# Turning the expert tiles' rows: DMA transposes on SyncE's queue in place of TensorE's, in a kernel of gated cross attention and a mixture of experts

## The chip, the cores and the metric

The kernel runs on one core of one Trainium2 chip. The metric is the device time of one execution in microseconds (us). A core has five engines that run at their own pace and meet at semaphores: TensorE (PE, matmuls and transposes, results in PSUM), VectorE (DVE), ScalarE (ACT), GpSimd (POOL) and SyncE (SP), which here only issues DMAs. Sixteen DMA engines move the data.

## The reference

```python
x = x + xattn(layernorm(x), ctx, ctx, ...)   # gated attention with decay, 8 heads, sequences of 128
x = x + ffn(layernorm(x), gate_w, w1, b1, w2, b2)

def ffn(x, gate_w, w1, b1, w2, b2):          # 4096 tokens, D=256, F=1024, 8 experts, the best 2 of them
    gate_scores = softmax(xf @ gate_w)
    topk_scores, topk_idx = top_k(gate_scores, 2)
    topk_scores = topk_scores / sum(topk_scores)
    h = gelu(einsum('td,edf->etf', xf, w1) + b1)
    y = einsum('etf,efd->etd', h, w2) + b2
    out = einsum('kt,ktd->td', topk_scores.T, y_sel)   # y_sel: y of the chosen experts
```

All arrays are float32.

## The kernel before

The kernel has two parts. In the first, up to about 250 us, eight steps of four sequences each go through the attention; each ends with the normed rows of 256 values and 16 more fields (token, gates) being scattered into a table in DRAM, `expert_rows`, sorted by expert. In the second part, which overlaps the last steps of the first, 39 tiles of table rows go through their expert: tiles 0 to 31 have 256 rows (`R`), tiles 32 to 38 have 128 that count.

Every engine has its own program, written out in order by hand; semaphores join them. There is no scheduler. Tile t passes through these stages:

- SP loads its rows (272 values each, `ROW`) from the table into one of four slots `xg[k]`, k = t mod 4 (`load`, the DMA on L523): three slots lie in `weight_stage`, the fourth in `v_centred_and_one`. Which rows, it reads from a list in SBUF, `rowi`.
- TensorE turns them: four 128x128 float32 transposes (two for a half tile) into PSUM (`turn_rows`, L1504), since layer 1 wants the 256 values along the partitions.
- DVE splits the turned rows into a high and a low float16 half (`split_rows`): a cast (L2087) and a subtraction (L2089), from PSUM into `xh[t mod 2]`, in the trace `x_slots`. The products of the halves give near float32 accuracy: three matmuls for one.
- TensorE does layer 1, 48 matmuls (L1519) into the bank group `scores`; ScalarE applies gelu in four quarters (L1038); DVE splits the result (L2096, L2098); TensorE does layer 2, 48 matmuls (24 for a half tile, L1533); DVE adds the bias and multiplies by the gate (L2105, L2111); POOL adds the rows to `out_rows` in DRAM by an indirect DMA (L663).

A "turn" t is one round of the tile loop: on TensorE it is the transposes of tile t+1, layer 1 of tile t and layer 2 of tile t-1, in this order; on DVE it is the split and the fields of tile t+1 (`row_fields`), the four gelu splits of tile t and the gating of tile t-1. So on DVE the split of tile t+1 comes behind the gating of tile t-2, which needs the end of TensorE's turn t-1. Turns 0 to 12 and the last ones are written out, 13 to 28 are a loop. Between the turns of DVE lie the routing of the last two attention steps (`choose`, `records`) and the list of the late tiles (`late_list0` to `late_list2`, between turns 6 and 9).

SP's program between its row loads: `write_x1(LAST)` writes the last attention result; after `next_rows(8)` come nine `clear`s (L488, 272 KB of zeros each, into the table's unused rows), then waits for the late list (`s_tl2`), for all scatters and for all clears (`s_clear`), then `next_rows(9)`. In the kernel before `next_rows(n)` loads tile n+4 as soon as tile n has been turned (`s_xT`) and its fields are read (`s_id`).

In code, the clears stand here:

```python
for n in range(3, EARLY - 4):        # EARLY = 13
    next_rows(n)
... # nine clears
sp.wait_ge(s_tl2, 2)
... # all scatters landed
sp.wait_ge(s_clear, 16 * (NE + 1))
for n in range(EARLY - 4, EARLY):
    next_rows(n)
```

Of the kernel before, what the change touches and what calls it, by code (L numbers as in the profile page):

```python
# [13 lines left out]
P = 128  # L14
R = 2 * P
# [32 lines left out]
def build(nc, x, ctx_in, igate_w, igate_b, fgate_w, fgate_b, out_w, gate_w, w1, b1, w2, b2, out):  # L48
# [51 lines left out]
    with ExitStack() as ctx:  # L100
# [3 lines left out]
        def sem(name):  # L104
            return ctx.enter_context(nc.semaphore(name))
# [249 lines left out]
        x_slots = [stage[:, :, :].rearrange("p a f -> p (a f)")[:, s * SLOT:(s + 1) * SLOT] for s in range(3)]  # L355
        xg = [x.rearrange("p (b w) -> p b w", w=ROW) for x in x_slots + [v_old[:, 0:SLOT]]]
        hf = E[:, 0:2, :, :].rearrange("p a c t -> p (a c t)")
        hh = [x.rearrange("p (w c t) -> p w c t", w=2, c=FC) for x in (
# [14 lines left out]
        s_xhi = sem("rows_high")  # L373
        s_xh = sem("row_halves")
        s_l1 = sem("layer1_quarter")
# [9 lines left out]

        L20, Y0, FREE0 = 1, 4, 3

        class Turn:
# [11 lines left out]
            def slot(self, ahead):  # L400
                return (self.u + ahead) % 4

            def landed(self, ahead, dmas=1):
# [10 lines left out]
        with nc.Block() as block:  # L414

            @block.sync
            def _(sp):
# [107 lines left out]

                def next_rows(t):
                    tr = Turn(0, t)
                    sp.wait_ge(s_xT, t + 1)
                    sp.wait_ge(s_id, t + 1)
                    load(tr, 4)  # L530

                def turn(tr, first, left):
                    if left > 4:
                        sp.wait_ge(s_xT, tr.t + 1)
                        sp.wait_ge(s_id, tr.t + 1)
                        load(tr, 4)

                write_x1(NEXT_LAST)
# [12 lines left out]
                next_rows(0)  # L551
                next_rows(1)
                next_rows(2)
                write_x1(LAST)
                for n in range(3, EARLY - 4):
                    next_rows(n)
# [549 lines left out]
            def _(pe):  # L1106
# [392 lines left out]
                run_steps(body, pe)  # L1499
                def turn_rows(tr, ahead):  # L1500
                    pe.wait_ge(s_gx[tr.slot(ahead)], tr.landed(ahead))
                    for c in range(KC):
                        for b in range(tr.rows(ahead) // P):
                            ins = pe.transpose(ps_xt[:, c * R + b * P:c * R + b * P + P],  # L1504
                                               xg[tr.slot(ahead)][:, b, c * P:(c + 1) * P], ident[:, :])
                    ins.then_inc(s_xT, 1)
# [36 lines left out]
                def tile_turn(tr, first, left, beside=()):  # L1543
# [9 lines left out]
                    if left > 0:  # L1553
                        expert = expert_of(tr.t)
                        pe.wait_ge(s_xh, tr.t + 1)
                        if left > 1:
                            turn_rows(tr, 1)
                        for q in range(4):
                            layer1(tr, expert, first, (q,))
                            routing()  # L1560
# [12 lines left out]
                pe.wait_ge(s_ee, NSTEP * (2 * SB))  # L1573
                turn_rows(Turn(0, 0), 0)
                stream_before(last, 3, 3)
# [16 lines left out]
            def _(dve):  # L1592
# [476 lines left out]
                def row_fields(tr, ahead):  # L2069
# [48 lines left out]
                def turn(tr, first, left, beside=()):  # L2118
                    if first:
                        row_fields(tr, 0)  # L2120
                        split_rows(tr, 0)
                    else:
                        expert = dve.value_load(exi[0:1, bass.ds(tr.t - 1, 1)], min_val=0, max_val=NE - 1)
                    if left > 1:
                        if not first:
                            dve.wait_ge(s_l1, tr.t * 4)
# [19 lines left out]
                row_fields(Turn(0, 0), 0)  # L2146
                split_rows(Turn(0, 0), 0)
                h_norm(last)
# [48 lines left out]
```

## Time and profile before

| | |
|---|---|
| median of three timed runs | 671.48 us (670.55 to 677.57) |
| span of the profiled execution, first to last instruction | 672.2 us |
| TensorE busy with matmuls | 626.9 us, 93% of the span |
| VectorE | 489.8 us, 73% |
| ScalarE | 323.3 us, 48% |
| GpSimd | 187.1 us, 28% |
| mean granted TensorE clock | 0.981 |

The profile comes from one execution; for it the page gives the span and no time of its own, so the span stands for it. Times in timelines count from its first instruction. Busy shares are means over stages that have different limits: in the attention all engines wait for each other in turn, in the tile loop from about 300 us on TensorE hardly pauses. Matmuls overlap in the array, and their ends are modelled, so the distance between starts says more than a row's own duration.

### The profile page before, as it was taken

The numbers are of one execution on the slowest core, as the hardware profiler recorded it, in microseconds if no ns is written. First come the engines' busy times: TensorE is split into PE (matmuls) and PEld (weight loads), VectorE is DVE, ScalarE is ACT, GpSimd is POOL, SyncE is SP. The second block draws the span as 40 slices with busy tenths as digits, with TensorE's granted clock in tenths as the row PEclk, the third lists the DMA queues.
The fourth block names the chain that finished last, engine by engine and source line by source line (L and its number), as shares of the span: only waits on it lengthen the run. The fifth ranks groups of instructions, "written<-read, shape, count | busy, mean of one in ns | idle before, by whom it ended". The sixth has DMA issues, their size and how long they took to land. (4 is left out here: it accounts for less than half of the span.)

```text
span 672.2 us, 20373 instructions
## 1 busy us (share of the span) xinstructions
PE 626.9 (93%) x6736; PEld 533.2 (79%) x6737; DVE 489.8 (73%) x1330; ACT 323.3 (48%) x767; POOL 187.1 (28%) x185
## 2 busy tenths in 40 slices
PE   1799998999889899999999999999999999999985
PEld 1567876778677668988989898988889898988774
DVE  2457988979889898985889866757675757666562
ACT  2668888777878746543332232323232323232321
POOL 3000003231323315135345332313141323233112
PEclk9899999969999999999999999999999999999998
DMA  4534537654644636333374423233232323133100
GB/s 139 156 106 148 160 94 231 188 189 144 207 152 137 199 103 208 77 70 78 66 221 93 68 40 61 43 56 46 46 52 44 57 39 64 35 65 53 21 4 1
DMA packets 55036, 66.55 MB, mean 99 GB/s; under 512 B 5472, under 2 KB 50720, under 8 KB 54832
## 3 DMA queue, kind: packets, MB, share of 16 engines
q1 hardware_dynamic: 41552, 48.13, 24.1%
q0 software_dynamic: 13296, 17.32, 14.1%
q8 instruction: 49, 0.80, 0.5%
q14 instruction: 27, 0.22, 0.1%
q10 hardware_dynamic: 112, 0.08, 0.1%
HBM read 41.50 MB, written 24.92 MB: 99 GB/s over the span
## 5 line engine op out<-in xcount | busy, mean ns | idle before, releaser
L1038 ACT ACTIVATE decay_slots<-scores,b_turned 128x256 f32<-128x256 f32 (+1 forms) x312 | 124.4, 451 | 257.4 <-PE scores L1519 244.9
L1519 PE MATMUL scores<-x_slots,w_halves 128*128 128x256 f16 (+1 forms) x1872 | 203.3, 264 | 0.8 <-issue 0.8
L1519 PEld LDWEIGHTS scores<-x_slots,w_halves 128*128 x1872 | 173.4, 98 | 23.3 <-issue 1.4
L641 POOL DMA_INDIRECT expert_rows<-xf_rows,slot_i x64 | 66.7, 1042 | 224.1 <-issue 114.8
L1533 PE MATMUL pv<-w_halves,decay_slots 128*128 x864 | 97.7, 273 | 0.0
L663 POOL DMA_INDIRECT out_rows<-v_centred_and_one,row_ids x36 | 57.8, 1605 | 138.8 <-DVE v_centred_and_one L2111 96.1
L1533 PE MATMUL gate_bank<-w_halves,q_and_k_halves 128*128 x840 | 95.0, 273 | 0.0
L1533 PEld LDWEIGHTS pv<-w_halves,decay_slots 128*128 128x128 f16 x864 | 84.1, 98 | 10.5 <-issue 0.3
L1533 PEld LDWEIGHTS gate_bank<-w_halves,q_and_k_halves 128*128 128x128 f16 x840 | 81.8, 98 | 10.1
L663 POOL DMA_INDIRECT out_rows<-work,row_ids x35 | 55.3, 1580 | 112.1 <-DVE work L2111 84.7
L1257 PEld LDWEIGHTS pv<-v_centred_and_one,decay_slots 128*128 128x128 f32 x512 | 64.5, 197 | 1.6
L1257 PE MATMUL pv<-v_centred_and_one,decay_slots 128*128 128x33 f32 x512 | 64.7, 262 | 0.0
L2098 DVE TENSOR_TENSOR decay_slots<-decay_slots 128x512 f16<-128x512 f32 (+1 forms) x80 | 51.2, 640 | 2.7
L2098 DVE TENSOR_TENSOR q_and_k_halves<-decay_slots,q_and_k_halves 128x512 f16<-128x512 f32 (+1 forms) x76 | 49.5, 652 | 2.6
L1705 DVE SCALAR_TENSOR_TENSOR w_halves<-weight_stage,w_halves 128x1024 f16<-128x1024 f32 x32 | 38.9, 1219 | 10.5 <-ACT w_halves L780 10.3
L768 ACT ACTIVATE decay_slots<-turn_bank 128x512 f32<-128x512 f32 x64 | 38.2, 597 | 10.7 <-PE turn_bank L1153 9.5
L1714 DVE SCALAR_TENSOR_TENSOR decay_slots<-scores,decay_slots 128x1024 f32<-128x1024 f32 x32 | 39.1, 1222 | 4.6 <-PE scores L1200 3.2
L2087 DVE CAST x_slots<-turn_bank 128x512 f16<-128x512 f32 (+1 forms) x39 | 25.1, 643 | 17.9 <-PE scores L1519 10.2
L1255 PE MATMUL pv<-minus_big_above,ident_bf 128*128 128x240 bf16 x128 | 34.9, 273 | 2.7 <-ACT work L789 1.6
L2096 DVE CAST decay_slots<-decay_slots 128x512 f16<-128x512 f32 (+1 forms) x80 | 33.5, 419 | 5.1 <-ACT decay_slots L1038 4.0
L780 ACT ACTIVATE w_halves<-weight_stage 128x1024 f16<-128x1024 f32 x32 | 33.7, 1055 | 3.4 <-DMA weight_stage<-in_L_ffn_w 3.4
L2096 DVE CAST q_and_k_halves<-decay_slots 128x512 f16<-128x512 f32 (+1 forms) x76 | 32.4, 426 | 1.2 <-ACT decay_slots L1038 0.8
(257 smaller groups left out, 845.5 us busy)
## 6 DMA issues: line engine op xcount, KB each, us to landing
weight_stage<-in_L_ffn_w SPq DMA_DIRECT2D x32, 512.0 KB
x_slots<-in_x SPq DMA_DIRECT2D x16, 512.0 KB
weight_stage<-expert_rows SPq DMA_DIRECT2D x30, 272.0 KB
ctx_slots<-in_ctx SPq DMA_DIRECT2D x8, 512.0 KB
out_rows<-x_slots SPq DMA_DIRECT2D x8, 512.0 KB
v_centred_and_one<-expert_rows SPq DMA_DIRECT2D x9, 272.0 KB
expert_rows<-v_centred_and_one SPq DMA_DIRECT2D x9, 272.0 KB
expert_rows<-xf_rows,slot_i POOLq DMA_INDIRECT x64
```

Of the source, the lines that this page charges most:

```text
L641: pool.indirect_dma_start(table, bass.IndirectOffsetOnAxis(ap=sloti[:, step[1], j, k:k + 1], axis=0), xfn[:, step[1], j, :], None, bounds_ ...
L663: pool.indirect_dma_start(out_rows, bass.IndirectOffsetOnAxis(ap=ids[:, k, b:b + 1], axis=0), yo[k][:, b, :], None, bounds_check=T - 1, oo ...
L768: act.activation(E[:, j, HG * r:HG * r + HG, :].rearrange("p c s -> p (c s)"), ps_t[:, :], ACT.Exp).then_inc(s_ee, 1)
L1038: ins = act.activation(hf[:, f * R:f * R + tr.rows(0)], ps_s[:, q, n * R:n * R + tr.rows(0)], ACT.Gelu, bias=b1T[:, bass.ds(expert, 1), f] ...
L1255: pe.matmul(ps_h[:, P + P + 16:512], ident_h[:, :], never[:, 0:120].unsqueeze(1).broadcast_to([P, 2, 120]), start=True, stop=True)
L1257: ins = pe.matmul(ps_h[:, h * (DH + 1):(h + 1) * (DH + 1)], E[:, j, k * KC + u, :], vaug[:, step[1], j, h, :], start=True, stop=True)
L1519: ins = pe.matmul(o, w, xh[:, tr.slot(0) % 2, b, k, 0:tr.rows(0)], start=(n == 0), stop=(n == 3 * KC - 1))
L1533: ins = pe.matmul(ps_y[k % 2][:, c * D:(c + 1) * D], hh[k % 2][:, a, f, c * P:(c + 1) * P], w, start=(f == 0 and n == 0 and c == 0), stop= ...
L1705: dve.scalar_tensor_tensor(out=lo, in0=stage[:, half, :], scalar=W_SCALE, in1=hi, op0=ALU.mult, op1=ALU.subtract).then_inc(s_lo, 1)
L1714: dve.scalar_tensor_tensor(out=c, in0=ps_s[:, :, 0:KC * P], scalar=QK_SCALE, in1=c, op0=ALU.mult, op1=ALU.mult).then_inc(s_cm, 1)
L2096: dve.tensor_copy(hi, src).then_inc(s_hhi, 1)
L2098: dve.tensor_tensor(lo, src, hi, ALU.subtract).then_inc(s_hh, 1)
```

## The change

The rows are now split as they lie, tokens along the partitions, and the float16 halves are turned afterwards. `split_rows` reads the slot `xg[k]` in SBUF, writes the high half into a buffer of its own (`xg_high`, two of them: the room of `out_w_rows`, which the attention no longer needs by then, and a spare piece of `weight_stage`) and the low half over the first part of the slot itself (`xg_low`). Then SP issues four DMA transposes a tile, each of 128 rows by 256 float16 values, from the two halves into `xh[t mod 2]`. Tile 0 alone still goes through TensorE. The halves are signalled by two semaphores `s_xh[0]` and `s_xh[1]`, 64 counts a tile. All tiles are split and turned at 256 rows, the last seven too. `next_rows(n)` on SP now first turns tile n+1, then loads tile n+4; `write_x1(LAST)` comes two calls earlier.

```diff
@@ names
+        xg_low = [x.bitcast(F16).rearrange("p (b w) -> p b w", w=2 * ROW)[:, :, 0:D]
+                  for x in x_slots + [v_old[:, 0:SLOT]]]
+        spare = stage[:, :, :].rearrange("p a f -> p (a f)")[:, 3 * SLOT:3 * SLOT + R // P * D // 2]
+        xg_high = [x.bitcast(F16).rearrange("p (b d) -> p b d", d=D) for x in (outw[:, :], spare)]
...
+        TURNED = 16 * 2 * (R // P)
...
+            def turned(self, ahead):
+                return (self.i * 2 + (self.u + ahead) // 2) * TURNED + TURNED
@@ SyncE
+                def turn_rows(tr, ahead):
+                    k = tr.slot(ahead)
+                    sp.wait_ge(s_xlo, tr.t + ahead)
+                    sp.sem_inc(s_held, 1)
+                    if not (isinstance(tr.t, int) and tr.t + ahead == 1):
+                        sp.wait_ge(s_l1, tr.t * 4 + (ahead - 1) * 4)
+                        sp.sem_inc(s_held, 1)
+                    for w, rows in enumerate((xg_high[k % 2], xg_low[k])):
+                        for b in range(R // P):
+                            sp.dma_start_transpose(out=xh[:, k % 2, w, :, b * P:b * P + P],
+                                                   in_=rows[:, b, :]).then_inc(s_xh[k % 2], 16)
+
+                def turn(tr, first, left):
+                    if left > 1:
+                        turn_rows(tr, 1)
+                    if left > 4:
+                        sp.wait_ge(s_xh[tr.slot(0) % 2], tr.turned(0))
+                        sp.sem_inc(s_held, 1)
+                        sp.wait_ge(s_id, tr.t + 1)
+                        sp.sem_inc(s_held, 1)
+                        load(tr, 4)
+
                 def next_rows(t):
-                    tr = Turn(0, t)
-                    sp.wait_ge(s_xT, t + 1)
-                    sp.wait_ge(s_id, t + 1)
-                    load(tr, 4)
...
+                    turn(Turn(0, t), False, NT)
...
                 next_rows(0)
-                next_rows(1)
-                next_rows(2)
                 write_x1(LAST)
-                for n in range(3, EARLY - 4):
+                for n in range(1, EARLY - 4):
                     next_rows(n)
@@ TensorE, tile_turn
-                        pe.wait_ge(s_xh, tr.t + 1)
-                        if left > 1:
-                            turn_rows(tr, 1)
+                        pe.wait_ge(s_xh[tr.slot(0) % 2], tr.turned(0))
@@ VectorE
                 def split_rows(tr, ahead):
-                    dve.wait_ge(s_xT, tr.t + (ahead + 1))
-                    n = tr.rows(ahead)
-                    src = ps_xt[:, :].rearrange("p (c t) -> p c t", c=KC)[:, :, 0:n]
-                    hi, lo = (xh[:, tr.slot(ahead) % 2, w, :, 0:n] for w in range(2))
+                    k = tr.slot(ahead)
+                    dve.wait_ge(s_gx[k], tr.landed(ahead))
+                    if not (isinstance(tr.t, int) and tr.t + ahead < 3):
+                        dve.wait_ge(s_xh[k % 2], tr.turned(ahead - 2))
+                    src, hi = xg[k][:, :, 0:D], xg_high[k % 2]
                     dve.tensor_copy(hi, src).then_inc(s_xhi, 1)
                     dve.wait_ge(s_xhi, tr.t + (ahead + 1))
-                    dve.tensor_tensor(lo, src, hi, ALU.subtract).then_inc(s_xh, 1)
+                    dve.tensor_tensor(xg_low[k], src, hi, ALU.subtract).then_inc(s_xlo, 1)
```

How the instructions stand at two places. First SP, behind the last clear (`expert_rows<-v_centred_and_one`). Before, the next instruction that waits is the row load of tile 13:

```order
L488 DMA expert_rows<-v_centred_and_one 128x2x272
L522 TENSOR_LOAD ctx_slots [waits rows_scattered11,empty_rows_cleared,rows_scattered10,rows_turned,rows_scattered01,ids_and_gates,rows_scattered00,late_tiles_listed]
L522 ISA x2
L523 ISA
L523 DMA weight_stage<-expert_rows 128x2x272
```

Now, in the same place, the transposes of tile 10 from its high half (`out_w_rows`) and its low half (`weight_stage`):

```order
L499 DMA expert_rows<-v_centred_and_one 128x2x272
L547 DMA_TRANSPOSE x_slots<-out_w_rows 128x2x128 [waits rows_scattered11,empty_rows_cleared,rows_scattered10,rows_low,rows_scattered01,late_tiles_listed,rows_scattered00,layer1_quarter]
L547 DMA_TRANSPOSE x_slots<-out_w_rows 128x2x128
L547 DMA_TRANSPOSE x_slots<-weight_stage 128x2x128 x2
L533 TENSOR_LOAD ctx_slots [waits row_halves_turned1,ids_and_gates]
L533 ISA x2
L534 ISA
L534 DMA weight_stage<-expert_rows 128x2x272
```

What moved: four transposes of tile 10 now stand between the clears and the row load, and the first of them carries the waits for clears, scatters and late list.

Second TensorE at the start of a turn: behind layer 2 (`pv` or `gate_bank`) it reads two entries of the expert list, then begins layer 1 (`scores`). Before:

```order
L1533 MATMUL pv<-w_halves,decay_slots 128x256 x4
L1541 TENSOR_LOAD ctx_slots
L1541 ISA x2
L1541 TENSOR_LOAD ctx_slots
L1541 ISA x2
L1504 MATMUL turn_bank<-ident,weight_stage 128x128 [waits rows_in1,row_halves]
L1504 MATMUL turn_bank<-ident,weight_stage 128x128 x3
L1519 ISA [waits gelu_quarter]
```

Now, at such a place:

```order
L1556 MATMUL gate_bank<-w_halves,q_and_k_halves 128x256 x4
L1564 TENSOR_LOAD ctx_slots
L1564 ISA x2
L1564 TENSOR_LOAD ctx_slots
L1564 ISA x2
L1542 ISA [waits gelu_quarter,row_halves_turned1]
L1542 MATMUL scores<-x_slots,w_halves 128x256 x2
```

What moved: the transposes are gone, and layer 1 itself waits for the landed halves of its tile.

## Rows read from the trace of the kernel before

**Rows 1.** The page: its first line.
```profile
span 672.2 us, 20373 instructions
```

**Rows 2.** Windows: PE, PEld, DVE, ACT, POOL busy; granted clock, DMA share, GB/s.
```profile
450.00:500.00 50.00, 49.95 (x458) 44.75 (x457) 32.05 (x75) 14.25 (x34) 13.06 (x9) 1.00 0.26 43
```

**Rows 3.** Groups by form, 284 to 606 us: two casts.
```profile
L2096 DVE CAST q_and_k_halves<-decay_slots 128x512 f16<-128x512 f32 x60 | 27.0, 450 | 0.1
...
L2087 DVE CAST x_slots<-turn_bank 128x512 f16<-128x512 f32 x28 | 19.4, 692 | 13.3 <-PE scores L1519 10.0 <-issue 2.3 <-DVE ctx_slots L2043 0.9
```

**Rows 4.** Timeline of a steady turn (start, duration, engine, line).
```profile
486.52 5.40 PE L1519 MATMUL scores<-x_slots,w_halves 128*128 128x256 f16 x48
...
489.87 1.55 POOL L663 DMA_INDIRECT out_rows<-work,row_ids  x1 [0.30 <-issue]
...
497.00 0.60 PE L1504 MATMUL turn_bank<-ident,v_centred_and_one 128*128 128x128 f32 x4
...
497.44 5.40 PE L1519 MATMUL scores<-x_slots,w_halves 128*128 128x256 f16 x48
...
499.76 0.69 DVE L2089 TENSOR_TENSOR x_slots<-turn_bank,x_slots 128x512 f16<-128x512 f32 x1
```

**Rows 5.** Timeline of the first turns, 254 to 286 us.
```profile
254.65 0.46 SPq L550 DMA_DIRECT2D q_and_k_halves<-in_L_ffn_b  x1
...
258.38 0.69 DVE L2089 TENSOR_TENSOR x_slots<-turn_bank,x_slots 128x512 f16<-128x512 f32 x1
...
262.18 0.63 PE L1504 MATMUL turn_bank<-ident,weight_stage 128*128 128x128 f32 x4 [0.43 <-issue]
...
269.46 0.69 DVE L2089 TENSOR_TENSOR x_slots<-turn_bank,x_slots 128x512 f16<-128x512 f32 x1
...
273.95 0.60 PE L1504 MATMUL turn_bank<-ident,v_centred_and_one 128*128 128x128 f32 x4
...
281.42 0.69 DVE L2089 TENSOR_TENSOR x_slots<-turn_bank,x_slots 128x512 f16<-128x512 f32 x1
...
285.26 0.60 PE L1504 MATMUL turn_bank<-ident,weight_stage 128*128 128x128 f32 x4
```

**Rows 6.** DMA issues: KB each and median us from issue to landing.
```profile
q_and_k_halves<-in_L_ffn_b SPq DMA_DIRECT2D x1, 1024.0 KB, 6.4
...
out_rows<-work,row_ids POOLq DMA_INDIRECT x35, 3.8
```

**Rows 7.** Timeline of turns 7 to 10: queue, splits, transposes.
```profile
338.90 0.38 SPq L523 DMA_DIRECT2D weight_stage<-expert_rows  x1
...
339.32 10.52 SPq L488 DMA_DIRECT2D expert_rows<-v_centred_and_one  x9
...
343.62 0.60 PE L1504 MATMUL turn_bank<-ident,weight_stage 128*128 128x128 f32 x4
...
350.83 0.69 DVE L2089 TENSOR_TENSOR x_slots<-turn_bank,x_slots 128x512 f16<-128x512 f32 x1
...
365.89 5.40 PE L1519 MATMUL scores<-x_slots,w_halves 128*128 128x256 f16 x48
```

**Rows 8.** Windows around the end of the clears.
```profile
350.00:352.00 2.00, 2.00 (x21) 1.80 (x19) 1.82 (x6) 0.49 (x2) 0.81 (x1) 1.00 0.62 215
```

**Rows 9.** Windows: granted clock after a stretch in which PE was idle.
```profile
26.81:28.60 1.79, 0.01 (x1) 0.00 (x0) 1.65 (x7) 1.57 (x4) 0.00 (x0) 1.00 0.76 262
28.60:29.23 0.63, 0.00 (x0) 0.00 (x1) 0.56 (x3) 0.13 (x1) 0.00 (x0) 0.51 0.16 54
29.23:35.00 5.77, 5.77 (x26) 4.39 (x27) 1.20 (x1) 2.97 (x6) 0.00 (x0) 0.50 0.31 91
```

**Rows 10.** Timeline of two of the last turns (tiles of 128 rows).
```profile
647.17 4.19 PE L1519 MATMUL scores<-x_slots,w_halves 128*128 128x128 f16 x48
...
648.52 0.42 DVE L2089 TENSOR_TENSOR x_slots<-turn_bank,x_slots 128x256 f16<-128x256 f32 x1
...
654.95 4.32 PE L1519 MATMUL scores<-x_slots,w_halves 128*128 128x128 f16 x48 [0.78 <-issue]
```

More of the change, by code:

```diff
@@ L373, in build @@
         s_xhi = sem("rows_high")
-        s_xh = sem("row_halves")
+        s_xlo = sem("rows_low")
+        s_xh = [sem(f"row_halves_turned{k}") for k in range(2)]
         s_l1 = sem("layer1_quarter")
@@ L524, in load @@
                         s_gx[k], 16)
-                def next_rows(t):
-                    tr = Turn(0, t)
-                    sp.wait_ge(s_xT, t + 1)
-                    sp.wait_ge(s_id, t + 1)
-                    load(tr, 4)
[L532 to L536, printed above, removed]
+                def turn_rows(tr, ahead):
[18 more added lines that the diff above has]
+                        load(tr, 4)
+                def next_rows(t):
+                    turn(Turn(0, t), False, NT)
                 write_x1(NEXT_LAST)
@@ L1499, in _, with turn_first_rows @@
                 run_steps(body, pe)
-                def turn_rows(tr, ahead):
-                    pe.wait_ge(s_gx[tr.slot(ahead)], tr.landed(ahead))
+                def turn_first_rows():
+                    pe.wait_ge(s_gx[0], 16)
                     for c in range(KC):
-                        for b in range(tr.rows(ahead) // P):
+                        for b in range(R // P):
                             ins = pe.transpose(ps_xt[:, c * R + b * P:c * R + b * P + P],
-                                               xg[tr.slot(ahead)][:, b, c * P:(c + 1) * P], ident[:, :])
+                                               xg[0][:, b, c * P:(c + 1) * P], ident[:, :])
                     ins.then_inc(s_xT, 1)
@@ L1573, in _ @@
                 pe.wait_ge(s_ee, NSTEP * (2 * SB))
-                turn_rows(Turn(0, 0), 0)
+                turn_first_rows()
                 stream_before(last, 3, 3)
@@ L2080, in row_fields, with split_first_rows @@
                     dve.tensor_tensor(gate[:, k, :], xg[k][:, :, F_SECOND], part[:, k, :], ALU.subtract).then_inc(s_id, 1)
-                def split_rows(tr, ahead):
-                    dve.wait_ge(s_xT, tr.t + (ahead + 1))
-                    n = tr.rows(ahead)
-                    src = ps_xt[:, :].rearrange("p (c t) -> p c t", c=KC)[:, :, 0:n]
-                    hi, lo = (xh[:, tr.slot(ahead) % 2, w, :, 0:n] for w in range(2))
+                def split_first_rows():
+                    dve.wait_ge(s_xT, 1)
+                    src = ps_xt[:, :].rearrange("p (c t) -> p c t", c=KC)
+                    hi, lo = (xh[:, 0, w, :, :] for w in range(2))
+                    dve.tensor_copy(hi, src).then_inc(s_xhi, 1)
+                    dve.wait_ge(s_xhi, 1)
+                    dve.tensor_tensor(lo, src, hi, ALU.subtract).then_inc(s_xh[0], TURNED)
+                def split_rows(tr, ahead):
+                    k = tr.slot(ahead)
[3 more added lines that the diff above has]
+                    src, hi = xg[k][:, :, 0:D], xg_high[k % 2]
                     dve.tensor_copy(hi, src).then_inc(s_xhi, 1)
                     dve.wait_ge(s_xhi, tr.t + (ahead + 1))
-                    dve.tensor_tensor(lo, src, hi, ALU.subtract).then_inc(s_xh, 1)
+                    dve.tensor_tensor(xg_low[k], src, hi, ALU.subtract).then_inc(s_xlo, 1)
                 def split_gelu(tr, q):
@@ L2118, in turn @@
                 def turn(tr, first, left, beside=()):
[L2119 to L2122, printed above, removed]
+                    if not first:
                         expert = dve.value_load(exi[0:1, bass.ds(tr.t - 1, 1)], min_val=0, max_val=NE - 1)
                     if left > 1:
-                        if not first:
-                            dve.wait_ge(s_l1, tr.t * 4)
                         split_rows(tr, 1)
@@ L2146, in _ @@
                 row_fields(Turn(0, 0), 0)
-                split_rows(Turn(0, 0), 0)
+                split_first_rows()
                 h_norm(last)
```

## The prediction, made before the changed kernel ran

> **What bounds the kernel now.** I read the windows first. In the steady turns TensorE (PE) is busy 49.95 of 50 us at a granted clock of 1.00, VectorE (DVE) 32.05, ScalarE 14.25, and the DMA engines have a share of 0.26 [rows 2]. So from 300 us on the end is set by what TensorE has to do, and its transposes are part of that. Then the timeline of one turn [rows 4]: layer 1 starts at 486.52 and again at 497.44, a turn of 10.92 us; the four transposes of the next tile's rows start at 497.00 and hold the array until 497.44, 0.44 us. Their end is modelled, so the gap to the next matmul is what counts, not the 0.60 of the row. In the same turn the low half of the split is done at 499.76 + 0.69 = 500.45, 3.45 us after the transposes start. Third, the timeline of the first turns and of turns 7 to 10, where DVE has routing and tile lists to work out and its split comes late [rows 5, 7]. Times are those of the profiled execution, whose span is 672.2 us [rows 1]; the timed median is 671.48, 0.7 less, and I take that off at the end.
>
> **What goes from TensorE.** Tiles 1 to 31 lose four transposes each, 31 x 0.44 = 13.6 us. Tiles 32 to 38 (128 rows, two transposes) lose at most half of that each; part of it lies in the pause that stays at the start of those turns (0.78 us before the turn at 654.95, which has no transposes at all [rows 10]), so I count 1.2 us for the seven. With everything hidden the change is worth 14.8 us: 656.7.
>
> **What the split costs.** The cast of 128x512 read PSUM in 692 ns; casts of that size from SBUF take 450 [rows 3], so each split ends 0.24 us earlier after it starts. The subtraction stays at 0.69. DVE is not the bound in a steady turn, so this only gives the transposes more time. In the last seven turns the split now handles 256 rows instead of 128: 0.45 + 0.69 instead of 0.42 + 0.42, 0.3 us longer beside idle DVE time.
>
> **What the DMA transposes cost.** No row shows one. Call q the time that the SyncE queue is held by one of 64 KB, and T the time from the end of the split to the landing of all four. For q the nearest row is the plain load from the same queue, 0.38 us [rows 7]; that is the low end. The high end is an indirect DMA whose descriptors GpSimd builds, 1.55 [rows 4] (its landing is 3.8 [rows 6]). For landing after the last issue: the nine clears stop issuing at 339.32 + 10.52 = 349.84, and in 350 to 352 the DMA share is 0.62, so traffic ends near 351.6, 1.8 us later [rows 7, 8]; the high end is 3.8. That gives T from 4 x 0.39 + 1.8 = 3.4 to 4 x 1.55 + 3.8 = 10.0. I take q = 0.6 and 2.2 for landing, **T = 4.6**: near the plain row, since queue and issuing engine are the same, and above it, since a plain copy is the least that a transposing one can be.
>
> Two pages of the Trainium skill point opposite ways. "VectorE: DVE Perf Modes", section "The three transpose paths", gives 1309 ns for a 128x128 transpose by DMA and 390 for one by TensorE; a tile has eight such blocks, one after the other an estimate of 10.5 us, which is the slow rival below; the trace has TensorE at 0.44 for all of a tile's f32 blocks. "DMA: Bandwidth & Descriptors", section "Latency and other measured facts", gives an effective 261 GB/s for transposes, so that a tile's 256 KB would move in an estimated 1.0 us and only issue and landing would count. No row of before decides between them.
>
> **Steady turns.** A turn becomes 10.48 us. The split ends 3.45 - 0.24 = 3.2 us into it, so the transposes have 7.3 us before layer 1 wants them. At T = 4.6 nothing waits. The row load of the tile three turns later, now behind the transposes on the queue, has turns to spare. Where T is over 7.3, layer 1 of a tile starts (3.2 + T) after the turn before the last ended, so two turns take 10.48 + 3.2 + T.
>
> **First turns.** Tile 1: the split would end near 258.8, and SyncE has just issued the 1 MB bias load, which lands 6.4 us after 254.65 [rows 5, 6]; by T or behind that load the halves are there at about 263.4, wanted at 262.18. From there turn 1 takes 273.95 - 262.18 - 0.44 = 11.3, so turn 2 starts layer 1 at 274.7 (before: 273.95 + 0.44 = 274.4); tile 2's halves are there at 270.15 - 0.5 + 4.6 = 274.3. Turn 3: 285.6 by TensorE, but tile 3's split ends at 282.11 - 0.24, and 4.6 later it is 286.5, against 285.7 before. So turn 4 starts about 0.4 us later than before instead of 1.8 earlier; turns 4 to 7 then gain 0.44 each: turn 8 starts **1.4 us earlier**.
>
> **Turn 10, the wait that the change adds.** SyncE's program has nine clears of 272 KB between the transposes of tile 9 and those of tile 10, and behind them it waits for the late tile list, all scatters and all clears. In before only row loads stood behind this, four tiles ahead. Now tile 10's transposes do, and layer 1 of turn 10 waits for them. In the time of the trace before, with turn 8 starting at 343.62 [rows 7]: tile 9's split ends at 351.52 - 0.24 = 351.28; four transposes 2.4 us; the load of tile 12 1.2 (10.52 / 9, what a lookup and an issue take among the clears); the first clear at 354.9; from first clear to last landing 351.6 - 339.3 = 12.3, so 367.2; then T: 371.8. Without a wait turn 10 would start at 343.62 + 2 x 10.48 = 364.6. **Stall: 7.2 us** (1.5 or so of it already at turn 9, whose halves come at 351.28 + 4.6 = 355.9, wanted at 354.1). Between the bounds of q and T it is 5.2 to over 11. What is late next is nothing: DVE and ScalarE catch up during the stall.
>
> A stall of this length also costs clock. TensorE is idle from 26.81 to 29.23; the granted clock is 1.00 until 28.6, 0.51 in the rest of the pause, and 0.50 for the 5.8 us of work from 29.23 to 35 [rows 9], the lower of its two levels, 1.2 GHz of 2.4. Layer 1 is dense matmuls, so 6 us at half speed do 3 us of work: **+3.0** (0 if the clock holds).
>
> **Sum.** Start of turn 10: -1.4 - 2 x 0.44 + 7.2 = +4.9; clock +3.0, so +7.9. Turns 10 to 30: 21 x 0.44 = -9.2. Last seven -1.2. Total **-2.5 us**: 669.7 for the profiled execution, 671.48 - 2.5 = **669.0** for the median.
>
> **Rivals.**
> A. The short one: q = 0.39, T = 3.4, clock unharmed. Turn 8 starts 2.6 earlier, the stall is 369.8 - 364.6 = 5.2, and 2.6 + 0.9 - 5.2 + 9.2 + 1.2 = 8.7 us are won: 662.8. Were the wait for the clears hidden altogether, it would be 656.7. For it: the DMA engines have 0.26 of share in a steady turn. Against it: the wait stands in the program order, and the clears alone are 12.3 us.
> B. Longer transposes, still inside a turn: q = 1.1, T = 7.0. First turns +2.8 at turn 4, +1.0 at turn 8, stall 11.6, clock 3: +14.7 at turn 10, -9.2 after. The last turns take 7.78 us now (647.17 to 654.95 [rows 10]) and split at 648.52 + 0.42; there two turns are 7.6 + 2.2 + 7.0, so 8.4 each, +3. Total +8.5: 680.
> C. Slower, by one mechanism: the chain split, four transposes, layer 1 is longer than the turn's 7.3 us and takes TensorE's place as the bound. It decides from T = 7.3. At T = 10.0, the top of the row bounds, two turns take 23.7, so +0.9 a turn instead of -0.4: about +7 in the first turns, +4 in turns 4 to 7, +15 from the stall, clock 3, +19 in turns 10 to 30, +13 in the last seven: +61, 732. At T = 8.5 the same sum gives about 705. For it: nothing shows what a transposing DMA takes, and the two accumulates of each turn (3.8 us to land) run just when it would. Against it: 7.3 us is more than any issue and landing of the plain rows add up to.
> D. That it doesn't do what it says: if the transposes' landing were hidden but TensorE's 0.44 us were only turned into another wait at the turn's start, nothing but the stall (371.8 against 365.5) and its clock would be left: 671.5 + 6.3 + 3.0 = 681. The steady windows (no idle TensorE, no wait named) speak against it.
>
> **Chances.** Forecast (T 4 to 5.5, stall and clock as above, 665 to 673) 0.40; A 0.25; B and times between it and the forecast 0.15; C 0.17; D 0.03. About 1% is what a measurement of this kernel can tell from no change, 664.8 to 678.2. Faster by more: A, 0.25. Within: the forecast and a third of B, 0.45. Slower: 0.30. The range must leave out at most 0.2: below, A's better half under 660 (0.06); above, the part of C from T = 8.5 (0.12). So 660 to 703.
>
> **What the profile after would show.** Right: layer 1 starts every 10.48 us between 400 and 600; four transposing DMAs on SyncE's queue after each split, landed well before the turn ends; one idle TensorE stretch of 5 to 8 us around 366, released by a DMA into the tile halves, with a granted clock of 0.5 behind it; waits of about 1 us at the starts of turns 1 and 3. Wrong: no idle stretch at turn 10 (the clears' wait was hidden), an idle TensorE before every tile (C), or a queue held over 1 us by a transpose (B). I would be most wrong by q, which enters T four times and the stall eight times.

## The result, and the profile of the changed kernel

The changed kernel takes 696.42 us (median of 4 runs, 694.34 to 699.54) against 671.98 us of the kernel before (4 runs beside it): a ratio of 1.0351, 95% interval 1.03 to 1.0402. It is 3.5% slower. The forecast of 669.0 was wrong in sign; the time lies inside the range.

The profiled execution took 699.54 us, its span is 697.5. A run's time was 2.0 us above its span here and in the runs below, so I compare spans with spans: 697.5 - 672.2 = +25.3 us. By the medians it is 24.4. The four executions of the changed kernel have spans from 692.3 to 697.5, and the profiled one is the longest. The head of the page, its DMA line, its costliest group and its sum over the groups of waits:

```profile
span 697.5 us, 20366 instructions
...
PEclk9899997999979998999999799999999999999998
...
DMA packets 98813, 76.54 MB, mean 110 GB/s; under 512 B 49248, under 2 KB 94496, under 8 KB 98608
...
L1542 PE MATMUL scores<-x_slots,w_halves 128*128 128x256 f16 (+1 forms) x1872 | 212.0, 272 | 32.4 <-DMA x_slots<-weight_stage 29.1
```

The waits of TensorE from 250 us on (in total, times, longest):

```profile
PE scores L1542 <- DMA x_slots<-weight_stage: 29.1, 12, 10.0
PE scores L1542 <- DMA x_slots<-v_centred_and_one: 1.9, 2, 1.6
```

Layer 1 waits 31 us for transposed halves, in 14 of 38 turns. The answer to [rows 4] is the timeline of a steady turn (start, duration):

```profile
500.47 0.69 DVE L2119 TENSOR_TENSOR weight_stage<-weight_stage 128x512 f16<-128x512 f32 x1
...
501.57 4.92 SPq L547 DMA_TRANSPOSE x_slots<-weight_stage  x4
...
507.63 0.40 SPq L534 DMA_DIRECT2D weight_stage<-expert_rows  x1
508.83 5.13 PEld L1542 LDWEIGHTS scores<-x_slots,w_halves 128*128 x48 [0.39 <-issue]
...
519.21 0.86 PEld L1542 LDWEIGHTS scores<-x_slots,w_halves 128*128 x8
519.32 0.93 PE L1542 MATMUL scores<-x_slots,w_halves 128*128 128x256 f16 x7
```

From 508.83 to 519.32 it is 10.49 us. The four transposing DMAs hold the queue for 4.92 us, 1.23 each; the plain load of 272 KB takes 0.40. From the end of the split (501.16) to the start of layer 1 (508.83) it is 7.7 us, but that is the slack and not T: no wait for a transpose is named here, and the 0.39 of waiting is no wait for one either. The run with two transposing DMAs a tile (e1_half, below) has the same 0.39 at its turn 21, with its transposes off the queue 5.0 us before:

```profile
483.66 2.33 SPq L547 DMA_TRANSPOSE x_slots<-weight_stage  x2
...
490.97 1.10 PEld L1542 LDWEIGHTS scores<-x_slots,w_halves 128*128 x11 [0.39 <-issue]
```

T can be read where layer 1 does wait for a transpose. In those 14 turns it starts 6.5 to 8.2 us after the split (turn 10: after the first issue), 7.1 in the middle: 5.0 to 6.5 us in which the four DMAs hold the queue, and 1.2 to 2.1 us from the end of the last issue. The forecast had 4.6.

The windows against [rows 2]: the DMA share is 0.48 in place of 0.26, and TensorE works 49.04 of 50 us; what is missing are the waits of turns 16 and 17 (0.73 and 0.23).

```profile
450.00:500.00 50.00, 49.04 (x448) 43.50 (x447) 32.07 (x77) 14.51 (x35) 15.98 (x9) 1.00 0.48 78
```

Turn 1, against [rows 5]: the bias load is issued at 254.88, the transposes behind it take 6.11 us, layer 1 starts at 267.03. Under it the windows around this (PE, PEld, DVE, ACT, POOL busy; granted clock; DMA share; GB/s):

```profile
259.18 6.11 SPq L547 DMA_TRANSPOSE x_slots<-weight_stage  x4
...
267.03 2.74 PE L1542 MATMUL scores<-x_slots,w_halves 128*128 128x256 f16 x12 [5.57 <-DMA x_slots<-weight_stage]
```

```profile
261.00:267.00 6.00, 0.46 (x5) 0.16 (x2) 5.83 (x9) 2.84 (x8) 3.00 (x3) 0.79 0.45 102
267.00:272.00 5.00, 4.97 (x28) 3.44 (x29) 0.89 (x2) 1.77 (x5) 1.57 (x3) 0.57 0.65 216
272.00:274.00 2.00, 2.00 (x39) 1.84 (x38) 1.69 (x4) 1.13 (x3) 0.00 (x0) 1.00 0.00 0
```

Turns 9 and 10, against [rows 7]: the transposes of tile 9, the nine clears, the transposes of tile 10.

```profile
359.64 0.69 DVE L2119 TENSOR_TENSOR weight_stage<-weight_stage 128x512 f16<-128x512 f32 x1
...
360.50 5.05 SPq L547 DMA_TRANSPOSE x_slots<-weight_stage  x4
...
366.67 0.39 SPq L534 DMA_DIRECT2D weight_stage<-expert_rows  x1
...
367.11 11.43 SPq L499 DMA_DIRECT2D expert_rows<-v_centred_and_one  x9
...
367.17 6.90 PE L1542 MATMUL scores<-x_slots,w_halves 128*128 128x256 f16 x48 [3.53 <-DMA x_slots<-weight_stage]
...
371.87 0.69 DVE L2119 TENSOR_TENSOR weight_stage<-weight_stage,out_w_rows 128x512 f16<-128x512 f32 x1
...
382.48 2.77 SPq L547 DMA_TRANSPOSE x_slots<-out_w_rows  x2
...
385.30 2.54 SPq L547 DMA_TRANSPOSE x_slots<-weight_stage  x2
...
389.32 2.95 PE L1542 MATMUL scores<-x_slots,w_halves 128*128 128x256 f16 x13 [10.01 <-DMA x_slots<-weight_stage]
```

```profile
379.30:389.30 10.00, 0.01 (x1) 0.00 (x0) 2.82 (x9) 0.00 (x0) 3.10 (x2) 0.73 0.62 105
389.30:395.00 5.70, 5.68 (x31) 4.19 (x32) 1.12 (x2) 1.20 (x3) 0.00 (x0) 0.57 0.41 97
395.00:396.00 1.00, 1.00 (x11) 0.90 (x10) 0.45 (x2) 0.53 (x3) 0.00 (x0) 1.00 0.05 4
```

Tile 10's split is done at 372.56 and its transposes are issued at 382.48. Of the waits that stand between, the one for the clears to land ended last (SyncE's own waits: in total, times, longest):

```profile
SPq L589 <- DMA expert_rows<-v_centred_and_one: 3.6, 1, 3.6
```

TensorE is idle for 10.01 us and then runs 5.7 us at a granted clock of 0.57. Of the last turns, against [rows 10], one of the long waits:

```profile
679.76 4.88 PE L1542 MATMUL scores<-x_slots,w_halves 128*128 128x128 f16 x48 [2.57 <-DMA x_slots<-weight_stage]
```

**Where the 25.3 us are.** From the start of layer 1 of one turn to that of another, after less before (turn 0 starts at 254.88 and 255.08, turn 38 at 679.76 and 654.95):

| turns | before | after | difference |
|---|---|---|---|
| start of turn 0 | 255.08 | 254.88 | -0.2 |
| 0 to 4 | 41.54 | 49.38 | +7.8 |
| 4 to 5 | 13.36 | 15.76 | +2.4 |
| 5 to 8 | 34.08 | 32.96 | -1.1 |
| 8 to 10 | 21.83 | 36.34 | +14.5 |
| 10 to 11 (low clock) | 10.92 | 12.83 | +1.9 |
| 11 to 31 | 218.92 | 212.06 | -6.9 |
| 31 to 38 | 59.22 | 65.55 | +6.3 |
| 38 to the end | 17.25 | 17.74 | +0.5 |

### The profile page after: what moved, and what is told of

It reads as the page before. It is cut to its first block and busy times, and to the rows that moved or that the text cites. A ratio compares the mean times of both kernels' runs of the same rounds, so it can differ in the third digit from the quotient of the medians.

```text
span 697.5 us, 20366 instructions
## 1 busy us (share of the span) xinstructions
PE 626.3 (90%) x6598; PEld 526.4 (75%) x6599; DVE 485.5 (70%) x1330; ACT 324.2 (46%) x767; POOL 196.0 (28%) x185
## 2 busy tenths in 40 slices
DMA packets 98813, 76.54 MB, mean 110 GB/s; under 512 B 49248, under 2 KB 94496, under 8 KB 98608
## 5 line engine op out<-in xcount | busy, mean ns | idle before, releaser
L1542 PE MATMUL scores<-x_slots,w_halves 128*128 128x256 f16 (+1 forms) x1872 | 212.0, 272 | 32.4 <-DMA x_slots<-weight_stage 29.1
L1542 PEld LDWEIGHTS scores<-x_slots,w_halves 128*128 x1872 | 177.6, 101 | 63.1 <-issue 38.9
L686 POOL DMA_INDIRECT out_rows<-v_centred_and_one,row_ids x36 | 61.4, 1707 | 163.4 <-DVE v_centred_and_one L2141 117.1
L1556 PE MATMUL pv<-w_halves,decay_slots 128*128 x864 | 97.7, 273 | 0.2 <-issue 0.2
L1556 PE MATMUL gate_bank<-w_halves,q_and_k_halves 128*128 x840 | 96.0, 273 | 0.7 <-issue 0.6
L1556 PEld LDWEIGHTS pv<-w_halves,decay_slots 128*128 128x128 f16 x864 | 84.2, 98 | 10.4 <-issue 0.3
L1556 PEld LDWEIGHTS gate_bank<-w_halves,q_and_k_halves 128*128 128x128 f16 x840 | 82.3, 98 | 11.2 <-issue 1.4
L686 POOL DMA_INDIRECT out_rows<-work,row_ids x35 | 59.3, 1694 | 106.7 <-DVE work L2141 79.6
L1280 PEld LDWEIGHTS pv<-v_centred_and_one,decay_slots 128*128 128x128 f32 x512 | 66.6, 202 | 1.7
L1280 PE MATMUL pv<-v_centred_and_one,decay_slots 128*128 128x33 f32 x512 | 66.7, 266 | 0.0
L2128 DVE TENSOR_TENSOR q_and_k_halves<-decay_slots,q_and_k_halves 128x512 f16<-128x512 f32 (+1 forms) x76 | 49.4, 650 | 2.6
L1169 PE MATMUL turn_bank<-pick_head,three_parts 96*128 96x512 bf16 x64 | 25.7, 401 | 4.3 <-DVE three_parts L1703 2.4
```

The source lines that it names most:

```text
L686: pool.indirect_dma_start(out_rows, bass.IndirectOffsetOnAxis(ap=ids[:, k, b:b + 1], axis=0), yo[k][:, b, :], None, bounds_check=T - 1, oo ...
L1280: ins = pe.matmul(ps_h[:, h * (DH + 1):(h + 1) * (DH + 1)], E[:, j, k * KC + u, :], vaug[:, step[1], j, h, :], start=True, stop=True)
L1542: ins = pe.matmul(o, w, xh[:, tr.slot(0) % 2, b, k, 0:tr.rows(0)], start=(n == 0), stop=(n == 3 * KC - 1))
L1556: ins = pe.matmul(ps_y[k % 2][:, c * D:(c + 1) * D], hh[k % 2][:, a, f, c * P:(c + 1) * P], w, start=(f == 0 and n == 0 and c == 0), stop= ...
L2128: dve.tensor_tensor(lo, src, hi, ALU.subtract).then_inc(s_hh, 1)
```

## The experiments

Single runs without rounds are compared by their spans with 697.5. The start of turn 0, which no edit here should move, lies between 248.7 and 256.5 us in the profiles, and the changed kernel's own spans differ by 5.2 us, of which 697.5 is the top. So one span says little below 5 us; distances between turns are steadier.

### The chain with two DMAs a tile in place of four

Only the high halves are turned, and layer 1 reads the high half where it would read the low one. So this kernel leaves out the low halves of the rows, and TensorE does as many matmuls as before.

```diff
-        TURNED = 16 * 2 * (R // P)
+        TURNED = 16 * (R // P)
-                    for w, rows in enumerate((xg_high[k % 2], xg_low[k])):
+                    for w, rows in enumerate((xg_high[k % 2],)):
...
-                                    ins = pe.matmul(o, w, xh[:, tr.slot(0) % 2, b, k, 0:tr.rows(0)], start=(n == 0),
+                                    ins = pe.matmul(o, w, xh[:, tr.slot(0) % 2, 0, k, 0:tr.rows(0)], start=(n == 0),
```

> Only the high halves are turned by DMA (two transposing DMAs a tile instead of four), and layer 1 multiplies the high half where it would take the low one, so the output leaves out the low halves of the rows; TensorE does as many matmuls as in the changed kernel. Theory Q (the time that four transposes hold SyncE's queue, 1.24 us each, plus 2.3 us of landing, is what layer 1 waits for): T falls from 7.3 to 4.8, the stalls of the last turns (6.3 us in sum against before) go, those of the first turns and of turns 9 and 10 shrink by 2.5 to 5 each: a span of 677 to 682. Rival W (only the place of the clears costs, the transposes' own length does not): the stall of turn 10 shrinks by at most 2.5 and the rest stays, 693 to 696.

Measured: 674.59 us, span 672.6, 24.9 less than the changed kernel and 4.4 below what was expected. On the queue, a pair takes 2.3 to 2.5 us:

```profile
547.19 2.31 SPq L547 DMA_TRANSPOSE x_slots<-weight_stage  x2
```

Layer 1 of turn 9 starts 4.0 us after its split, that of turn 10 3.7 us after the first issue: a T somewhat under the prediction's 4.6. From turn 8 to turn 10 this kernel takes 28.7 us (344.21 to 372.89); the prediction had 28.2 (343.62 to 371.8). The terms, measured against forecast: 11.5 against 11.3 us to the first clear, 13.5 against 12.3 from there to the transposes, 3.7 against 4.6 to layer 1. So the model of the stall held to about a microsecond a term, and what it was fed for the transposes did not.

### Per DMA or per byte

Eight DMAs of 128x128 (32 KB) move the same bytes:

```diff
-                            sp.dma_start_transpose(out=xh[:, k % 2, w, :, b * P:b * P + P],
-                                                   in_=rows[:, b, :]).then_inc(s_xh[k % 2], 16)
+                            for c in range(KC):
+                                sp.dma_start_transpose(out=xh[:, k % 2, w, c, b * P:b * P + P],
+                                                       in_=rows[:, b, c * P:c * P + P]).then_inc(s_xh[k % 2], 16)
```

> Eight transposing DMAs of 128x128 a tile instead of four of 128x256, the same bytes. If the queue is held per DMA (a fixed price of 1.24 us), T is 8 x 1.24 + 2.3 = 12.2, two turns take 10.48 + 3.2 + 12.2, 12.9 each, and the span is 770 to 800. If it is held per byte (0.62 us each), T and the span stay where they are, 695 to 700. In between: a fixed part f and a part by bytes, f = 2 x q(32 KB) - 1.24.

Measured: 817.55 us, span 815.6, above the 770 to 800 that a price per DMA was expected to give and far from the 695 to 700 of a price per byte. Four of them take 5.06 us, 1.27 each, for half the bytes of those above:

```profile
539.39 5.06 SPq L548 DMA_TRANSPOSE x_slots<-v_centred_and_one  x4
```

The other way: the high half of a tile in one DMA of 128x512 (128 KB), the low half in two as before.

```diff
+                        if w == 0:
+                            sp.dma_start_transpose(out=xh[:, k % 2, w, :, :, :].rearrange("p b c t -> p (b c) t"),
+                                                   in_=rows.rearrange("p b d -> p (b d)")).then_inc(s_xh[k % 2], 16)
```

> Three transposing DMAs a tile: the high half in one of 128x512 (128 KB), the low one in two as before. Layer 1 reads the tile in two pieces of 128 columns instead of 256 in a row. If the queue is held per DMA, T falls by 1.24 to 6.1 and the span to about 688; if per byte, the large one holds it 2.5 us and the span stays at 695 to 700.

Measured: 688.16 us, span 686.1. The 128 KB take 1.24 us (L547), the two of 64 KB behind them 1.26 each (L551):

```profile
547.57 1.24 SPq L547 DMA_TRANSPOSE x_slots<-out_w_rows  x1
548.86 2.52 SPq L551 DMA_TRANSPOSE x_slots<-weight_stage  x2
```

The span of 686.1 is near the 688 expected. A transposing DMA held the queue for 1.21 to 1.26 us in the median at 32, 64 and 128 KB alike; single ones took from 0.9 to 2.7. The price is per DMA. A price per byte is ruled out by both runs.

### Two DMAs a tile

The low half is packed without gaps in its slot, so each half goes in one DMA of 128x512.

```diff
-        xg_low = [x.bitcast(F16).rearrange("p (b w) -> p b w", w=2 * ROW)[:, :, 0:D]
+        xg_low = [x.bitcast(F16)[:, 0:R // P * D].rearrange("p (b d) -> p b d", d=D)
-        TURNED = 16 * 2 * (R // P)
+        TURNED = 16 * 2
```

> Two transposing DMAs a tile, one for each half (128x512, 128 KB each): the low half is written side by side at the start of its slot, so that each half is one row of 512 values in a partition. Same work, half the DMAs. The runs so far held the queue 1.24 to 1.27 us per DMA for 32, 64 and 128 KB alike, so T should fall from 7.3 to 2 x 1.25 + 2.3 = 4.8, as in the run with only the high halves: 673 to 677. If the landing of 128 KB takes clearly longer than that of 64 KB, 680 to 688.

Measured: 678.87 us (676.26 to 681.0, 4 runs), ratio to the kernel before 1.01 (1.006 to 1.0139), span 677.2. A tile's two transposes take 2.36 us:

```profile
571.92 2.36 SPq L546 DMA_TRANSPOSE x_slots<-weight_stage  x2
```

Two issues fewer a tile are worth 17.6 us by the medians (696.42 to 678.87); the time came out 2 us above what was expected. The waits for transposes that are left are 7.35 us at turn 10, 3.53 at turn 1, 2.51 at turn 7, 1.48 at turn 34, 1.21 at turn 9 and three under 0.8.

### Which tiles pay

In these kernels a list of tiles keeps TensorE's transposes, and so the order of before; the rest is the changed kernel with four DMAs a tile.

```diff
+        BY_PE = (0,) + tuple((9, 10))
...
-                    if left > 1:
+                    if left > 1 and not by_pe(tr, 1):
                         turn_rows(tr, 1)
...
@@ TensorE
                         pe.wait_ge(s_xh[tr.slot(0) % 2], tr.turned(0))
+                        if left > 1 and by_pe(tr, 1):
+                            turn_rows(tr, 1)
```

The other two lists are (1, 2, 3) and tiles 32 to 38. Tiles 9 and 10:

> The changed kernel (four DMAs a tile) with tiles 9 and 10 turned by TensorE. Theory: stalls of 3.5 and 10.0 us and some 3 us at the low clock go, a stall of about 3 at turn 11 comes, since tile 11's transposes are now the first behind the clears: 685 to 689. If the loss before turn 11 is only moved to another place, 693 or more.

Measured: 684.49 us, span 682.5, 15.0 less than the changed kernel, 2.5 below what was expected. From turn 8 to turn 12 it takes 48.7 us (351.80 to 400.49), the changed kernel 59.7 (352.98 to 412.63) and the kernel before 43.7: 11.0 of the 16.0 us that were lost there come back, and turn 11 now waits 3.54. The rest of the 15.0 lies in turns that are the same in both programs (turn 0 alone starts 2.7 us earlier). So the wait behind the clears, with its clock, is the largest single loss.

Tiles 1 to 3:

> Tiles 1, 2 and 3 keep TensorE's transposes beside tile 0; all others are turned by four transposing DMAs as in the changed kernel. Theory (each first turn pays for its own late transposes, and the wait at turn 10 is a thing apart): the loss of the first turns, 7.6 us by the start of layer 1 of turn 4, goes nearly whole, so the span falls from 697.5 to 689 to 692 us, with the wait of turn 10 still about 10 us. Rival (the first turns are late because four transposes of any tile do not fit beside the load of the first weights, and the lateness only moves to tile 4): the span stays at 694 to 698.

Measured: 689.39 us, span 687.4, 10.1 less, 1.6 below what was expected. From turn 0 to turn 4 it takes 42.4 us (256.50 to 298.86) against 49.4, 7.0 of the 7.8 back. Turn 4 to 5 takes 13.7 against 15.8, although tiles 4 and 5 are turned as in the changed kernel. The wait at turn 10 is 8.45 us. The lateness does not move on to tile 4, where 1.68 us are waited.

Tiles 32 to 38:

> Tiles 32 to 38 keep TensorE's transposes beside tile 0; all others are turned by four transposing DMAs. Theory (the short last turns cannot hold casts and four transposes of 1.24 us): the waits of the last turns, 2.3 to 2.6 us each in the changed kernel, go, and the span falls from 697.5 by 5 to 6 us to 691.5 to 693. Rival (something else of the last turns is late too, the rows' loads behind results on the queue): a fall under 2 us, 695.5 to 698.

Measured: 687.73 us, span 685.8, 11.7 less where 5 to 6 were expected. From turn 31 to the end it takes 75.1 us (610.68 to 685.8), the changed kernel 83.3, the kernel before 76.5: 8.2 are the tiles' own. The other 3.5 lie elsewhere, in turns that are the same in both programs (turn 0 starts 1.3 us earlier, turns 0 to 10 take 2.7 less), and are put down to the scatter between executions. The rival is ruled out.

All three groups together, with four DMAs elsewhere (tiles 1, 2, 3, 9, 10 and 32 to 38 by TensorE):

> Tiles 1, 2, 3, 9, 10 and 32 to 38 are turned by TensorE as before, the other 26 (4 to 8, 11 to 31) by DMA. Theory Q: the places where the split ends late or the turn is short are taken out, all the rest hides; 26 x 0.44 = 11.4 us of TensorE are saved, less some 2 us of small waits in the steady turns: 661 to 664, faster than both kernels. Rival B (DMA engines shared with row loads and accumulates slow every turn): no better than before, 670 to 676.

Measured: 672.32 us (669.87 to 679.18, 10 runs), ratio 1.0036 (0.9998 to 1.0075), span 667.9. Missed by 8 us at the median, by 4 in the profiled execution, which is the fastest of the ten (spans from 667.9 to 677.2); what the slower ones lose no profile shows. The time is the rival's, its mechanism is not seen: steady turns take 10.48 us here too. The first tile behind the clears is now tile 11, and turn 11 waits in turn 10's place. Its transposes on the queue, and its layer 1:

```profile
371.31 2.50 SPq L551 DMA_TRANSPOSE x_slots<-weight_stage  x2
373.85 2.55 SPq L551 DMA_TRANSPOSE x_slots<-v_centred_and_one  x2
```

```profile
378.35 7.03 PE L1546 MATMUL scores<-x_slots,w_halves 128*128 128x256 f16 x48 [3.02 <-DMA x_slots<-v_centred_and_one]
```

Two more waits of 1.75 and 1.30 us stand at tiles 4 and 6, T being 6.8 and 7.2 at turns 6 and 11.

### A version that is faster

Two DMAs a tile, and tiles 1, 2, 3, 9, 10 and 11 by TensorE:

> As the run with two DMAs a tile, but tiles 1, 2, 3, 9, 10 and 11 (late splits, and the clears on the queue) are turned by TensorE. T of 4.8 fits everywhere else; 25 x 0.44 + 1 us are saved, one wait of about 1 us in the last turns: 660 to 665, faster than both kernels. If contention on the DMA engines costs the rest, 669 to 673.

Measured: **664.35 us** (661.56 to 667.29, 6 runs), ratio to the kernel before 0.9892 (0.9858 to 0.9927), span 662.5. It beats both kernels, the one before by 1.1%. Waits for transposes are left at turn 7 (1.75 us), turn 34 (2.17) and turn 38 (0.78). Steady turns take 10.48 us, and layer 1 doesn't wait in them:

```profile
502.03 5.40 PE L1545 MATMUL scores<-x_slots,w_halves 128*128 128x256 f16 x48
...
512.51 5.40 PE L1545 MATMUL scores<-x_slots,w_halves 128*128 128x256 f16 x48
```

The other way to keep the transposes out of the clears is to change SyncE's order. Here all tiles but 0 go by DMA, two a tile, and tiles 10 and 11 are turned between the clears, ahead of the wait for them to land:

```diff
...
+                clear_expert(0)
+                next_rows(8)
+                for e in range(1, 4):
+                    clear_expert(e)
+                turn_only(9)
+                for e in range(4, 6):
+                    clear_expert(e)
+                turn_only(10)
+                for e in range(6, NE):
+                    clear_expert(e)
```

> As the run with two DMAs a tile (all tiles but 0 by DMA), but the nine clears are spread between the transposes of tiles 8 to 11, and the transposes of tiles 10 and 11 no longer stand behind the wait for the clears, only the row loads do. If the wait behind the clears is what costs at turn 10, 7 to 9 us (stall and low clock) come back against the run before: 665 to 669. If the clock or the DMA traffic itself costs there, no more than 3.

Measured: 670.06 us (665.94 to 674.51, 10 runs), ratio 0.9977 (0.9948 to 1.0007), span 663.9: 8.8 us below the same transposes behind the clears by the medians, where 7 to 9 were expected, and no gain over the kernel before that can be told. Turn 9 waits 2.38 us and turn 10 not at all; turns 8 to 10 take 25.2 us (339.65 to 364.84) in place of 29.9 (347.36 to 377.21), and turn 10 to 11 10.5 in place of 12.1. That is 6.3 of the 8.8.

Last, both together, with tiles 1, 2, 3, 9 and 33 by TensorE:

> Two transposing DMAs of 128x512 for each tile, the clears spread between the transposes of tiles 8 to 11, and TensorE's transposes for tiles 0, 1, 2, 3, 9 and 33. Theory (what is left above 10.48 us a turn in the version with two DMAs and tiles 1, 2, 3, 9, 10, 11 by TensorE are single waits of 1.75 and 2.17 us and the TensorE work of tiles 10 and 11): 660 to 663 us, 1 to 3 below that version's 664.35. Rival (small waits only move to the next late tile): 664 to 667.

Measured: 664.58 us (662.45 to 671.88, 6 runs), ratio 0.9887 (0.9828 to 0.9947), span 663.3. No better than 664.35, as the rival said, though not by its mechanism alone. The waits of turns 7 and 34 were there in the version above (1.75 and 2.17 us) and are there still (1.46 and 2.66): tile 33, which TensorE now turns, was not late, and tile 34 was. New is the wait of 2.00 us at turn 10, whose tile goes by DMA again:

```profile
329.77 5.41 PE L1567 MATMUL scores<-x_slots,w_halves 128*128 128x256 f16 x48 [1.46 <-DMA x_slots<-v_centred_and_one]
```

```profile
363.82 7.08 PE L1567 MATMUL scores<-x_slots,w_halves 128*128 128x256 f16 x48 [2.00 <-DMA x_slots<-weight_stage]
```

## Why the prediction was wrong

**The step that failed is the value taken for q**, the time that a transposing DMA holds SyncE's queue: 0.6 us "near the plain row, since queue and issuing engine are the same". It is 1.24. Four of them hold it for 5.0 us and more and not 2.4, so T was 6.5 to 8.2 where layer 1 waited for it, not 4.6; the other half of T, from the last issue to layer 1, was 1.2 to 2.1 against 2.2. T lay inside the bounds of 3.4 and 10.0, and the value came from the wrong neighbour: queue and engine were the same as the plain load's, the kind of DMA was not, and that sets the price. The indirect DMA's 1.55 was the nearer row. Halving the number of transposing DMAs, at the same bytes, took 17.6 us off the time.

**By the prediction's own sums, q gives the sign and about half of the miss.** With q = 1.24 and T = 7.0 they give 2.8 us at turn 4, 1.0 at turn 8, a stall of 12.1 and 15.3 us at turn 10, 9.2 less from there, and 4.3 in the last turns: +10 in place of -2.5. Rival B was this, at 680; the measured time is 16 us above it. That it lies inside the range says little for the sums: the range reached up to 703 for rival C, whose bound (T over 7.3 in every turn) the steady turns do not show. The kernel with two DMAs a tile tests the rest, since its T (4.1 to 5.9 us where layer 1 waited before turn 11) is near the forecast's. Against the forecast it lost 3.1 us more from turn 0 to turn 4 (45.0 us, 41.5 before), 1.9 more from turn 4 to turn 8 and some 2 more in the last turns, and came out right from turn 8 to 11 (+9.2 against +8.9) and in the steady turns (-8.3 against -8.8). So beside q the forecast of the first turns was wrong too; its model of the stall was right.

**TensorE's 0.44 us a turn: right.** Steady turns take 10.48 to 10.49 us, twenty turns from 11 to 31 gained 6.9 of 8.8 us, most of the rest lost at turns 16 and 17, where the queue was held for 5.8 and 6.3 us. The cast from SBUF took 0.43 us (0.45 forecast).

**The wait behind the clears: right in place and kind, 7.2 us forecast, 3.5 + 10.0 measured.** Counted from turn 8's start to turn 10's, 28.2 were forecast and 36.3 measured. Tile 9's own four transposes push the first clear back by 2.65 (5.05 against 2.4); from the first clear to the transposes of tile 10 it is 15.4 against 12.3 (issuing 11.43 against 10.52, landing 3.9 against 1.8); and from their first issue to layer 1 6.8 against 4.6. So 4.9 of the 8 us are q's. The other 3 are the clears': in e1_half, e3_three, e5_two, e9_pe_first and e10_pe_last, which keep this order, issuing took 10.6 to 12.0 and landing 2.5 to 3.2, and no run isolates the reason.

**The clock: right.** 0.57 for 5.7 us behind the stall; 3.0 us forecast, 1.9 + 0.44 at turn 10. What was left out is that there are more such places: turn 9's layer 1 took 6.90 in place of 5.40, turn 1's first quarters ran at 0.57.

**First turns: wrong, +0.4 at turn 4 forecast, +7.8 measured,** all but 0.8 of it undone by turning tiles 1 to 3 on TensorE. I had tile 1's halves at 263.4; they came at 267.03, since four transposes took 6.11 us beside the bias load, 1.53 each. The 5.57 us of idle TensorE then cost clock, which the prediction counted for turn 10 only: turns 1 to 2 took 14.05 us against 11.73. Turn 4 to 5 lost 2.4 more in three pauses for which the profile names no releaser (0.89 us at L1295, 0.64 at L1556, 0.69 at L1542); no transpose is waited for there, and in the runs with two DMAs (e1_half, e5_two) and in e10_pe_last this turn took 12.9 to 13.1 us. The cause stays open.

**Last turns: wrong, -1.2 forecast, +6.3 measured.** The prediction's own rule for two turns is 7.6 + the end of the split + T. The pairs from turn 34 and from turn 36 took 17.2 and 17.7 us, with splits that ended 3.0 and 2.7 us into a turn (2.2 assumed) and T of 6.5 and 7.0, against 15.8 and 15.6 before. The rule was right; the forecast didn't need it at T = 4.6. Rivals B and C did, and their sums for the seven turns are short: 8.4 in place of 7.78 us each is +4.3, not +3, and 9.9 is +15, not +13. One more slip, in the first turns: tile 2's split is put 0.5 us earlier, where the faster cast gives 0.24. None of these changes the sign of the forecast.

**Blocks, bytes or DMAs.** The Trainium skill, "VectorE: DVE Perf Modes", section "The three transpose paths", gives 1309 ns for a 128x128 transpose by DMA. A DMA of one such block held the queue for 1.23 us, which agrees; the estimate of 10.5 us for a tile took this as a price per block, and a DMA of two or of four blocks held the queue no longer than a DMA of one. By the rate in the Trainium skill, "DMA: Bandwidth & Descriptors", section "Latency and other measured facts", the 256 KB of a tile are an estimated 1.0 us; the four DMAs held the queue for 5.0 us and layer 1 could start after 6.5 at the least, so bytes were not what counted here.

## What to carry to other kernels

A transposing DMA cost its queue about 1.24 us here from 32 to 128 KB alike: count the DMAs between the data and its reader, and make one of 128x512 where there were two of 128x256. Set that chain against the slack of every stage by itself: the first and last rounds, and those with other work on the producing engine, have less of it than the steady ones. A distance between a producer and its reader is slack, and the length of the chain only where the reader is shown to wait for it. Moving data-dependent work onto a queue moves it behind everything that the queue already waits for; what stays on the engine at those few places (here six tiles of 39, beside tile 0) can decide the sign.

## What the runs showed of the hardware

- The queue time of a transposing DMA from SBUF to SBUF was 1.21 to 1.26 us in the median for 32, 64 and 128 KB, with single ones from 0.88 to 2.68; a plain load of 272 KB on the same queue took 0.38 to 0.40.
- The transposes come as small packets: under 512 B there were 5472 packets before and 49248 after, and the DMA share of a steady window (450 to 500 us) rose from 0.26 to 0.48 (0.44 in the version with two DMAs a tile and six tiles by TensorE, 0.37 where only one half is turned).
- Some pauses of TensorE cost more than their length. One of 2.00 us (e11_two_best, turn 10) was followed by a layer 1 of 7.08 us in place of 5.40, at a granted clock of 0.72 (363.8 to 369.8 us), one of 3.53 us (changed kernel, turn 9) by one of 6.90, at 0.69 (367.2 to 372.2). But behind pauses of 2.51 us (e5_two, turn 7) and 2.08 us (e2_eight, turn 9), as behind 1.46 us (e11_two_best, turn 7), the clock stayed at 1.00 and layer 1 took 5.41 us. The length of the pause alone does not tell which it will be, and no run isolates what does.
